# Queries' softmax one turn later, low halves in another instruction form, scatters dealt out differently: one change to a graph network kernel

## The reference, cut to what matters

```python
x = x + segment_max_part(xn, src, dst) + attention_mlp(xn)          # layer 0
x = x + moe(layernorm(x))     # 8 experts: 3 products each, relu, weighted by a gate
xn = layernorm(x)
x = x + sage(xn, edge_index) + linear_attention(xn)                 # layer 1
#   sage: three times  mean over in-edges @ Wl + h @ Wr
#   linear_attention: q = softmax(q, over the 32 dims of a head) * 32**-0.5
x = x + capacity_ffn(layernorm(x))
```

## Time and profile before

| what | value |
|---|---|
| median of 3 runs | 2121.96 us (2119.42 to 2125.1) |
| the profiled execution | 2125.89 us, its span 2124.0 us |
| mean granted TensorE clock | 0.834 of full speed |
| PE busy | 1649.1 us, 78% |
| DVE busy | 1212.6 us, 57% |
| POOL busy | 1118.2 us, 53% |
| ACT busy | 534.6 us, 25% |

### The profile page before, as it was taken

One profiled execution on the slowest core, in us unless ns is written; L12 is line 12 of the kernel. 1 busy time (PEld: TensorE's weight loads), 2 busy tenths in 40 slices (PEclk: granted clock), 3 DMA queues, 4 the chain that ended last, 5 costly groups with the idle time before them and its releaser, 6 DMA issues. The chain is left out here.

```text
span 2124.0 us, 23931 instructions
## 1 busy us (share of the span) xinstructions
PE 1649.1 (78%) x7942; PEld 979.8 (46%) x7942; DVE 1212.6 (57%) x2743; ACT 534.6 (25%) x839; POOL 1118.2 (53%) x882
## 2 busy tenths in 40 slices
PE   7994656255544586999999977759998998999377
PEld 6971222122212364555555556525556555655255
DVE  6877777667667455777777755614444122344621
ACT  4001011101101123666666634400012001100042
POOL 0768878888787687888888878830000000000065
PEclk9556877677776666999999977779999999999678
DMA  6356788888787522121212110045423544476121
GB/s 184 80 138 178 196 233 219 221 218 224 212 216 206 139 61 38 36 33 35 34 33 34 11 41 2 2 105 130 108 74 76 132 123 96 136 188 161 58 67 29
DMA packets 200470, 239.15 MB, mean 113 GB/s; under 512 B 69342, under 2 KB 177257, under 8 KB 195121
## 3 DMA queue, kind: packets, MB, share of 16 engines
q1 hardware_dynamic: 127809, 177.07, 31.9%
q0 software_dynamic: 71920, 60.43, 12.8%
q10 hardware_dynamic: 654, 0.56, 0.1%
HBM read 150.80 MB, written 86.24 MB: 112 GB/s over the span
## 5 line engine op out<-in xcount | busy, mean ns | idle before, releaser
L718 POOL DMA_INDIRECT adjacency<-all_cell_val,all_cell_idx x400 | 531.3, 1328 | 133.1 <-issue 121.3
L284 POOL DMA_INDIRECT edge_ring<-b_rows,all_src_idx x400 | 495.3, 1238 | 186.9 <-issue 169.5
L1612 PE MATMUL bank<-w_big,w_zh 125*128 125x448 f16 x1050 | 371.2, 354 | 26.0 <-DMA w_big<-adjacency 26.0
L1612 PE MATMUL bank<-w_big,w_zl 125*128 125x448 f16 x1050 | 371.0, 353 | 0.0
L2002 POOL DMA_INDIRECT ffn_rows<-x_rows,ffn_idx x13 | 15.8, 1214 | 625.0 <-DVE ffn_idx L1887 621.4
L538 DVE SCALAR_TENSOR_TENSOR edge_ring<-edge_ring,w_keep 125x256 f32<-125x256 f32 x399 | 193.1, 484 | 122.3 <-DMA edge_ring<-b_rows,all_src_idx 104.4
L1087 ACT ACTIVATE bank<-bank,w_shift,w_scale 128x448 f32<-128x448 f32 x224 | 147.1, 697 | 76.3 <-PE bank L728 76.3
L1612 PEld LDWEIGHTS bank<-w_big,w_zh 125*128 125x128 f16 x1050 | 102.9, 98 | 124.1 <-DMA w_big<-adjacency 26.2
L1612 PEld LDWEIGHTS bank<-w_big,w_zl 125*128 125x128 f16 x1050 | 102.9, 98 | 99.7 <-issue 6.9
L693 DVE SCALAR_TENSOR_TENSOR edge_junk<-bank,all_key_c,all_later 125x400 f16<-125x400 f32 x232 | 145.6, 628 | 0.0
L728 PE MATMUL bank<-all_yn,w_W1h 128*128 (+1 forms) x448 | 123.4, 357 | 10.3 <-DVEq L1123 10.3
(11 more groups left out here) (464 smaller groups left out, 3170.8 us busy)
## 6 DMA issues: line engine op xcount, KB each, us to landing
w_big<-adjacency SPq DMA_DIRECT2D x104, 490.0 KB
run_max<-edge_ring SPq DMA_DIRECT2D x40, 1120.0 KB
adjacency<-edge_zero SPq DMA_DIRECT2D x25, 714.0 KB
experts_gb<-gate_rows SPq DMA_DIRECT2D x56, 224.0 KB
edge_ring<-b_rows,all_src_idx POOLq DMA_INDIRECT x400, 7.0
adjacency<-all_cell_val,all_cell_idx POOLq DMA_INDIRECT x400, 2.7
w_big<-adjacency SPq DMA_DIRECT2D x104, 56.9 KB
run_max<-edge_ring SPq DMA_DIRECT2D x40, 130.0 KB
```

The lines of the kernel that those rows point to most:

```text
L284: nc.gpsimd.indirect_dma_start(ring[:, k % RING, :], None, dram.rows[:, :], bass.IndirectOffsetOnAxis(ap=c.src_idx[:, k:k + 1], axis=0)).t ...
L718: nc.gpsimd.indirect_dma_start(dram.adj_flat, bass.IndirectOffsetOnAxis(ap=c.cell_idx[:, k:k + 1], axis=0), c.cell_val[:, k:k + 1], None). ...
L1612: ins = mm(ps[4 * b + h][:, 0:T], z[:, g * JG + j, half(h)], adj[g][:, j, :], start=(g == 0 and j == 0 and z is zh), stop=False)
```

## The change

Five edits. (1) `edges`, PE: two `grams` for each `degrees`, the remaining `degrees` at the end; DVE: scans are interleaved from the fifth one-hot round on, so that 51 instead of 24 are done at the last. (2) Six scatters move to the end of `edges`; their indices are made at scan 350. (3) The borders are shifted: `edges` 0 to 5, `join_norm_gate` 6 to 61 (56 as before), `experts` 62 to 323 (262 instead of 242), `between` 324 to 399 (76 instead of 102). (4) Low halves and one addition are written as `scalar_tensor_tensor` with a factor 1.0 instead of `tensor_tensor`. (5) `between`: the softmax of group t-2 instead of t-1 in turn t, its parts placed between other work; all rows leave PSUM by ACT.

```diff
-JOINED = 56
+EDGED, JOINED, EXPERT = 6, 62, 324
+    scans_by = lambda g: 3 * max(g - 4, 0) if g < 13 else 27 + 2 * (g - 13)
 # edges, POOL, after the last gather
+                pool.wait_ge(first_made, 1)
+                pool.wait_ge(zeroed, 32 * NB)
+                place_cells(nc, c, dram, pool, 0, EDGED)
 # edges, PE
                 for j in range(NB):
                     grams(j)
+                    if j % 2:
+                        degrees(j // 2)
+                for j in range(NB // 2, NB):
                     degrees(j)
 # edges, DVE
-                    if g >= 13:
-                        scan(2 * (g - 13))
-                        scan(2 * (g - 13) + 1)
+                    for k in range(scans_by(g), scans_by(g + 1)):
+                        scan(k)
...
-                        step(v.tensor_tensor(c.xT[:, :, at(t)], c.xT[:, :, at(t)], sx[:], ALU.add))
+                        step(v.scalar_tensor_tensor(c.xT[:, :, at(t)], sx[:], 1.0, c.xT[:, :, at(t)], ALU.mult, ALU.add))
+                    if k == L - 50:
+                        dve.wait_ge(counted, EDGED + 2)
+                        make_cells(v, count_step, c, cell0[:], dup0[:], slice(0, EDGED))
+                        dve.sem_inc(first_made, 1)
 # experts, DVE (the same for c.el in join_norm_gate and c.yl in between)
-                            v.tensor_tensor(hwl[:, f % 2], h2[:, f % 2], hwh[:, f % 2], ALU.subtract).then_inc(dw, 1)
+                            v.scalar_tensor_tensor(hwl[:, f % 2], h2[:, f % 2], 1.0, hwh[:, f % 2], ALU.mult, ALU.subtract).then_inc(dw, 1)
 # between, ACT: after zh of the turn, before the square roots
+                    if 2 <= t <= G4 + 1:
+                        q = rows[:, WC * (t - 2):WC * (t - 2) + size(t - 2), 0:H]
+                        act.wait_ge(q_less, t - 1)
+                        a(q, q, ACT.Exp).then_inc(q_exp, 1)
...
-                        for j in blocks(t - 1)[0::2]:
-                            qkv_even(j)
+                        for j in blocks(t - 1):
+                            rows_out(j)
 # between, DVE: after k_max
+                        mx, q, over = q_of(g)
+                        step(v.tensor_reduce(mx, q, AX.X, ALU.max))
+                        v.tensor_tensor(q, q, over, ALU.subtract).then_inc(q_less, 1)
 # between, DVE: after 1/deviation, in place of the first odd row
+                    if t >= 2:
+                        mx, q, over = q_of(t - 2)
+                        dve.wait_ge(q_exp, t - 1)
+                        step(v.tensor_reduce(mx, q, AX.X, ALU.add))
+                        step(v.reciprocal(mx, mx))
+                        step(v.tensor_scalar(mx, mx, HD1 ** -0.5, None, ALU.mult))
+                        v.tensor_tensor(q, q, over, ALU.mult).then_inc(q_norm, 1)
-            experts(nc, c, w, dram, made, lambda pool: place_cells(nc, c, dram, pool, JOINED, 298, made))
+            experts(nc, c, w, dram, made, lambda pool: place_cells(nc, c, dram, pool, JOINED, EXPERT, made))
```

More of the change, by code:

```diff
@@ L172, in edges @@
         own_col = s.sb("own_col", [B, 1])
+        cell0, dup0 = s.sb("cell0", [B, EDGED]), s.sb("dup0", [B, EDGED])
         with ExitStack() as early:
@@ L212, in edges @@
         scanned, ends_turned, ends_scanned, ends_back = s.sem("scanned"), s.sem("ends_turned"), s.sem("ends_scanned"), s.sem("ends_back")
-        counted, own_c = s.sem("counted"), s.sem("count_steps")
+        counted, own_c, first_made = s.sem("counted"), s.sem("count_steps"), s.sem("first_cells_made")
         pe_done, act_done, mixed = s.sem("mix_pe"), s.sem("mix_act"), s.sem("mix_steps")
@@ L564, in _ @@
                 v.reciprocal(rdeg[:], rdeg[:]).then_inc(rd, 1)
-                for k in range(24, 30):
+                for k in range(scans_by(NH), 53):
                     scan(k)
@@ L597, in _ @@
                 v.tensor_copy(carry_t[:], ps[7][0:NB, 3 * P:3 * P + B]).then_inc(part_out, 1)
-                for k in range(30, 38):
+                for k in range(53, 56):
                     scan(k)
@@ L612, in _ @@
                 ins.then_inc(att_v, 1)
-                for k in range(38, 44):
+                for k in range(56, 58):
                     scan(k)
@@ L623, in _ @@
                 ins.then_inc(att_v, 1)
-                for k in range(44, SCANS):
+                for k in range(58, SCANS):
                     scan(k)
@@ L911, in _ @@
                         dve.wait_ge(scaled, g + 1)
-                        v.tensor_tensor(c.el[:, :, at(g)], y[:, g % 2, :, 0:wide(g)], c.eh[:, :, at(g)], ALU.subtract).then_inc(lowed, 1)
+                        v.scalar_tensor_tensor(c.el[:, :, at(g)], y[:, g % 2, :, 0:wide(g)], 1.0, c.eh[:, :, at(g)], ALU.mult, ALU.subtract).then_inc(lowed, 1)
                     if 3 <= t < G4 + 2:
@@ L1227, in qkv @@
                     if j >= 2:
-                        pe.wait_ge(odd_out if j % 2 else even_out, j // 2)
+                        pe.wait_ge(qkv_out, j - 1)
                     product3(nc, ps[5 + j % 2][0:B, 0:3 * H], [(c.yh[:, k, tok(j)], c.yl[:, k, tok(j)]) for k in range(KH)],
@@ L1238, in _ @@
                         g = t - 2
[L1239 to L1240 removed]
+                        pe.wait_ge(qkv_out, WC * g + size(g))
                         if g:
@@ L1310, in split, with rows_out @@
                     a(hi, src, ACT.Copy, scale=WS).then_inc(split_high, 1)
-                def qkv_even(j):
+                def rows_out(j):
                     act.wait_ge(qkv_done, j + 1)
                     act.wait_ge(r_ready, j // WC + 1)
-                    a(rows[:, j, 0:3 * H], ps[5][0:B, 0:3 * H], ACT.Identity, scale=r[:, j:j + 1]).then_inc(even_out, 1)
+                    a(rows[:, j, 0:3 * H], ps[5 + j % 2][0:B, 0:3 * H], ACT.Identity, scale=r[:, j:j + 1]).then_inc(qkv_out, 1)
                 for t in range(G4 + 3):
@@ L1343, in _ @@
                         nc.scalar.copy(c.yh[:, :, at(t)], y[:, :, at(t)]).then_inc(high, 1)
[L1344 to L1347, removed]
                     if t == 0:
@@ L1368, in _, with q_of @@
                 step = Steps(dve, own)
-                def qkv_odd(j):
-                    dve.wait_ge(qkv_done, j + 1)
-                    v.tensor_scalar(rows[:, j, 0:3 * H], ps[6][0:B, 0:3 * H], r[:, j:j + 1], None, ALU.mult).then_inc(odd_out, 1)
+                def q_of(g):
+                    mx = qm[:, WC * g:WC * g + size(g), :]
+                    return (mx, rows[:, WC * g:WC * g + size(g), 0:H].rearrange("p j (h d) -> p j h d", d=HD1),
+                            mx.unsqueeze(3).to_broadcast([B, size(g), HEADS1, HD1]))
                 def low(n):
@@ L1416, in _ @@
                         ins.then_inc(scaled, 1)
-                    if 1 <= t <= G4:
-                        for j in blocks(t - 1)[3:]:
-                            qkv_odd(j)
                     if t < G4:
@@ L1422, in _ @@
                         dve.wait_ge(scaled, t + 1)
-                        v.tensor_tensor(c.yl[:, :, at(t)], y[:, :, at(t)], c.yh[:, :, at(t)], ALU.subtract).then_inc(lowed, 1)
+                        v.scalar_tensor_tensor(c.yl[:, :, at(t)], y[:, :, at(t)], 1.0, c.yh[:, :, at(t)], ALU.mult, ALU.subtract).then_inc(lowed, 1)
                         dve.wait_ge(rs_ready, t + 1)
@@ L1435, in _ @@
                         v.tensor_tensor(ml[:], w.mqkv[:], mh[:], ALU.subtract).then_inc(m_low, 1)
[L1436 to L1441, removed]
-                        dve.wait_ge(odd_out, (WC * g + size(g)) // 2)
-                        step(v.tensor_reduce(mx, q, AX.X, ALU.max))
-                        v.tensor_tensor(q, q, over, ALU.subtract).then_inc(q_less, 1)
                     if 1 <= t < len(pieces):
                         low(t)
-                    if 1 <= t <= G4:
-                        dve.wait_ge(q_exp, t)
-                        step(v.tensor_reduce(mx, q, AX.X, ALU.add))
-                        step(v.reciprocal(mx, mx))
-                        step(v.tensor_scalar(mx, mx, HD1 ** -0.5, None, ALU.mult))
-                        v.tensor_tensor(q, q, over, ALU.mult).then_inc(q_norm, 1)
                 dve.wait_ge(w.loaded, w.total)
@@ L2138, in build @@
                 w.adj_in = [g.sem(f"adj0_in{n}") for n in range(SG)]
-                between(nc, c, dram, w, z, rows, f, qT, ctx, (first, rest), lambda pool: place_cells(nc, c, dram, pool, 298, L))
+                between(nc, c, dram, w, z, rows, f, qT, ctx, (first, rest), lambda pool: place_cells(nc, c, dram, pool, EXPERT, L))
             fold = halves[:, NB * T:NB * T + NP]
```

11 lines of the change are left out of this document (4 added, 7 removed).

## The result

| | median | runs |
|---|---|---|
| before | 2123.53 us | 4, 2119.42 to 2126.52 |
| after | 2101.18 us | 4, 2099.42 to 2103.54 |

The ratio is 0.9892, with a 95% interval of 0.9875 to 0.9908: 22 us less. The forecast was 2100. The profiled execution of after took 2099.42 us, its span is 2097.4 us, its mean granted clock 0.853 of full speed.

What follows compares the result with a forecast made beforehand. POOL was taken to bound edges and between, PE to bound experts. Edges -12.6 and the adjacency load -9.6 (late start of between, shorter path) made 22.2 us off 2122.0: 2100 predicted, own range 2091 to 2107, 8-in-10 range 2071 to 2113.

Steps and rivals of the forecast that it cites:

- Edges, -12.6 forecast: In edges, all of POOL's stops for PE go and the gather chain shifts 12.6 us earlier.
- Rival (C): In edges, gathers wait for ring slots as DVE starts the MLP late; 12.6 us lost, 2112 us; chance 0.06.
- The six scatters, "nothing": At the end of edges, their 8.9 us fit in POOL's 13.38 us wait for the next stage and cost nothing.
- The new form, nothing: Low halves as scalar_tensor_tensor hold a scatter as before; the edit costs nothing, the whole 40 us of holds being the other end.
- rival (A): The new form frees the scatters, so 262 fit in experts: 2075 us; chance 0.20.
- 1254.1 forecast for POOL's end: In experts, 262 scatters don't fit; POOL ends 24.9 us after the 1241.8 that ended the stage, before the edges gain.
- the others' path: 127.1 forecast: In between, the path of the engines other than POOL falls from 142.1 to 127.1 us, a gain of 15.
- no turn can gain more than the 5.05: In between, a turn's gain is limited to the 5.05 us of softmax and weight piece at its end.
- (B): Turns of between don't get shorter, as ACT gets all rows and both table loads: 2115 us; chance 0.07.
- (D): Turns of between get longer at the square roots, +22 us on (B): 2137 us; chance 0.03.
- POOL's 120.9: In between, POOL's 76 scatters up to the adjacency load take 120.9 us, bounds 115.2 and 127.5.
- the load issued at ctx_done, not behind a scatter: Sign in the profile after: at the end of between, POOL's scatters no longer determine when the adjacency load is issued.

Runs made afterwards that it cites:

- e8: The kernel after with the experts/between border at 305 and the new order of grams, degrees and scans in edges undone: 2115.15 us, ratio to before 0.9946.
- e1: The kernel after with the low halves and the one addition written as tensor_tensor again: 2100.73 us, ratio to before 0.9884.
- e2: The kernel after with the softmax and rows edit in between undone, border still at 324: 2123.58 us, ratio to before 1.0007.
- e3: e2 with the border between experts and between at column 305 instead of 324: 2102.80 us, ratio to before 0.9901.
- e4: The kernel after with the border between experts and between at column 305 instead of 324: 2104.46 us, ratio to before 0.9912.
- e10: The kernel after with the experts' gated value kept in its PSUM bank and the border at 332: 2078.24 us, ratio to before 0.9783.
- e11: The kernel after with the experts' gated value kept in its PSUM bank and the border at 326: 2072.64 us, ratio to before 0.9752.
- e5: The kernel after with the low half of the queries' experts made for one column of each half only: 2074.79 us, ratio to before 0.9770.
- e9: e2 with 16 extra PE products in each turn of between, before the variances: 2118.77 us, ratio to before 0.9971.

## Why the prediction was right, and where it was not

**Edges, -12.6 forecast.** Right in mechanism, and near in size: all stops gone, the last gather at 668.9 against "near 670". 11.5 us are left at the next stage and 10.3 at the first scatter of `experts` (826.16 against 836.45), the cost of the six scatters in them. The later scans cost no gather: DVE waited 100.1 us for gathers, against 104.4 in the earlier trace rows. Alone the edit gave 10.2 us. Rival (C) falls.

**The six scatters, "nothing".** Mis-sized by 2 us (16.82 against 14.6 to 15.0, above). The prediction gave them no gain of their own; with POOL's chain setting the load, the 8.9 us that they take out of it are part of the gain, and e8 shows it (-11.5 us with edit (1) undone). They end at 679.1 and the next gather comes 6.55 us behind them: with POOL last the stage closes later, as at the next border.

**The new form, nothing.** Right; rival (A) is refuted by the earlier trace rows, the rows of after, and e1.

**Experts.** 1254.1 forecast for POOL's end, 1255.9 measured, PE idle before it as said. The border then took 4.6 instead of 1.3 us, which I had taken from the end behind DVE in the earlier trace rows. `between` started at 1260.5, not 1255.4.

**Between, the others' path: 127.1 forecast, 118.2 measured.** This is the term that was mis-sized most. The square root came 7.0 us into the turn (6.9 forecast) and the scaling could start at 9.65, but "scaling y starts at 10.7 now and waits for PE's spread, so this is hidden" failed: the spread ended at 8.25, PE running at the full clock of 2.4 GHz, and what y waited for was DVE's own moved softmax. The extra 0.9 us for a fourth row was not there either: that row was out of PSUM at 10.8 and y scaled at 10.9, and the copy of y started at 10.9, not 13.6. So a turn took 14.2 us, not 16.9, and "no turn can gain more than the 5.05" was wrong: it bounded the moved work and left the clock of the rest at what it had been. From the first centring to the last, six turns gained 28.5 us (17.5 forecast, for five). Before the first, 1.1 us were lost, and the end lost 29.9 - 26.4 = 3.5 us (3 forecast): together 23.9 us and not 15. Rivals (B) and (D) fall.

**What bounds the load.** I had the others 6 us behind POOL's 120.9; POOL took 1380.55 - 1260.46 = 120.1, and as the path was 118.2, POOL ended the stage. So "the load issued at ctx_done, not behind a scatter" is wrong. Two errors nearly cancel: 5 us too early at the border, and 7 us too long behind it (127.2 against 120.1). The load was forecast at 1395.2 - 12.6 = 1382.6 and came at 1380.55. The time is right partly by this luck. The profiled execution, which the sum was made for, was forecast at 2103.7 and took 2099.4.

**The table loads.** By the Trainium skill ("ScalarE: Activation LUTs", section "What ACT_TABLE_LOAD costs") a drain of about 1.38 us comes with each load. The prediction's estimate from that page was a total of about 2107. The trace does not agree: 0.01 us from the exponential's load (ends 1325.46) to the exponential (1325.47), and 0.02 to the square root. Ahead of each load it is 0.02 us as well.

**What the prediction did not see.** It priced the softmax edit at 15 of 22 us. At this border the edit is worth 22 us (e2), at a border where POOL's list fits beside the experts none (e3, e4). The rows had said so the earlier trace rows: if POOL ends `between` by 19.5 us, a faster pipeline there gains nothing; it only repays what 20 more scatters cost in `experts`, 25 us in the forecast.

## What to carry to other kernels

When one engine's list of work runs through several stages, add that list up over all of them before the stages are looked at one by one. As long as that engine ends the stages, moving its items between stages where it is busy all the time is worth nothing; filling its idle time, or taking holds out of it, is worth most of what it saves there (here 10.2 of 12.6 us for the stops, and 26 of 31 us for the holds). And when a forecast shortens a pipeline, ask what PE's clock does when its pauses shrink.

## What the runs showed of the hardware that was not expected

- A stage that POOL ends with scatters closes late: DVE begins the next one 3.8 us (e10) and 4.6 us (after) behind the end of the last scatter, against 1.3 us behind DVE's own end. In e11 DVE ended 1.1 us after the last scatter, and the next stage still began only 4.8 us behind that scatter. What fills the time stays open.
- A scatter that POOL issues is held by a long DVE instruction with both inputs in SBUF (2.08 us instead of 1.19, in either form) and not by one with an input in PSUM (1.19 us beside L1153 in e11). Here this was worth 26 us (e5) to 30 us (e11) of 2101.
- PE at 41 to 42 us busy of 50 was granted 0.74 of its clock in the old order, a mixture of its levels of 1.2 and 2.4 GHz, and 1.00, all of it at 2.4 GHz, in the new, where the turns are shorter. Before the old order's variances PE had stood for 4.45 us, and they took 3.52 us. In the last four full turns of e9, behind the extra products, they took 3.52 after a pause of 3.14 us, then 2.39, 1.91 and 1.91 after pauses of 2.71; in after it is 1.91, after pauses of 0.47.
